# Edge stage of a graph network on Trainium2: groups of six whole buckets instead of 512 slots, and row numbers turned by TensorE instead of through memory

## The reference

```python
def _L1_gnn_ref(h, row, col, dist, eW1, eb1, eW2, eb2, nW1, nb1, nW2, nb2):
    edge_in = jnp.concatenate([h[row], h[col], dist], axis=1)
    e = jax.nn.silu(edge_in @ eW1 + eb1)
    e = jax.nn.silu(e @ eW2 + eb2)
    agg = jax.ops.segment_sum(e, row, num_segments=h.shape[0])
    node_in = jnp.concatenate([h, agg], axis=1)
    out = jax.nn.silu(node_in @ nW1 + nb1) @ nW2 + nb2
    return out
h = jnp.maximum(_layernorm(x, axis=-1), 0.0)
x = x + _L0_gnn_ref(h, edge_index, L0_gnn_W1, L0_gnn_b1, L0_gnn_W2, L0_gnn_b2)
h = jnp.maximum(_layernorm(x, axis=-1), 0.0)
x = x + _L1_gnn_ref(h, src, dst, edge_weight1, ...)
```

## Time and profile before

| what | number |
| --- | --- |
| median of three runs | 9332.65 us |
| profiled execution | 9347.07 us |
| its span in the trace | 9345.3 us |
| mean granted clock of TensorE | 0.972 |
| TensorE busy | 8577.7 us (92%) |
| TensorE, weight loads | 7679.0 us (82%) |
| VectorE busy | 7760.4 us (83%) |
| ACT busy | 5344.2 us (57%) |
| GpSimd busy | 2985.7 us (32%) |

### The profile page before, as it was taken

How to read it: one execution, slowest core, us unless ns; L and a number is a source line. 1 busy time by engine, 2 the same in 40 slices (tenths; PEclk the granted TensorE clock), 3 DMA queues, 4 the chain that set the end, 5 groups by cost and what they waited for, 6 DMA issues and landing times. The chain is left out here.

```text
span 9345.3 us, 289343 instructions
## 1 busy us (share of the span) xinstructions
PE 8577.7 (92%) x95106; PEld 7679.0 (82%) x95890; DVE 7760.4 (83%) x21596; ACT 5344.2 (57%) x14224; POOL 2985.7 (32%) x4177
## 2 busy tenths in 40 slices
PE   3999999999999989998888999599999999999997
PEld 2777777777777769998888998489989899999895
DVE  8999999999999976775888886478888888888884
ACT  3777777777777750001777786245555555555552
POOL 5877777777777830000000000011111111111110
PEclk9999999999999999997999998599999999999998
DMA  2666666666666677664999997533333333333332
GB/s 74 149 150 149 152 148 152 148 151 148 151 148 151 149 172 193 190 190 114 228 222 211 240 241 168 129 98 92 97 93 92 97 91 97 93 94 97 89 97 72
DMA packets 1475613, 1312.43 MB, mean 140 GB/s; under 512 B 829932, under 2 KB 1211094, under 8 KB 1473636
## 3 DMA queue, kind: packets, MB, share of 16 engines
q1 hardware_dynamic: 1444438, 1270.13, 56.3%
q0 software_dynamic: 28224, 26.62, 1.1%
q10 hardware_dynamic: 1840, 0.53, 0.0%
HBM read 777.40 MB, written 361.77 MB: 122 GB/s over the span
## 5 line engine op out<-in xcount | busy, mean ns | idle before, releaser
L621 POOL TENSOR_SCALAR OH<-iot,kd 128x102 bf16<-128x102 bf16 x3440 | 2334.1, 698 | 61.7 <-PE S L753 61.4
L2170 POOL DMA_INDIRECT Qx<-tab_q,tidx x294 | 407.5, 1386 | 5231.9 <-DVE skt L2204 2602.0
L1425 PE MATMUL wp<-AF,XS 128*128 128x256 f32 x9604 | 1214.6, 285 | 157.5 <-issue 121.7
L1425 PEld LDWEIGHTS wp<-AF,XS 128*128 128x128 f32 x9604 | 1165.9, 191 | 189.0 <-issue 188.8
L911 ACT ACTIVATE RB<-PS 128x256 int16<-128x256 f32 x2401 | 898.6, 381 | 639.9 <-PE PS L779 591.6
L1451 ACT ACTIVATE AF<-RG 128x1536 fp32r<-128x1536 uint8 x686 | 1022.6, 1491 | 340.9 <-PE wp L1425 208.0
L794 PE MATMUL HP<-T3a,RB 128*128 128x193 bf16 x9604 | 1187.3, 246 | 27.3 <-ACT RB L911 27.3
L753 PE MATMUL S<-LH,OHf 128*102 128x256 f32 (+14 forms) x6860 | 1160.5, 316 | 50.3 <-ACT LH L875 29.6
L2191 ACT ACTIVATE Z<-Zb 128x512 f32<-128x512 f32 x882 | 556.2, 631 | 991.6 <-DVE Zb L2249 987.6
L875 ACT ACTIVATE LH<-LB,pl 128x128 f32<-128x128 bf16 (+14 forms) x4116 | 1113.1, 356 | 0.0
L753 PEld LDWEIGHTS S<-LH,OHf 128*102 128x102 f32 x6860 | 921.7, 169 | 195.9 <-issue 96.1
(11 more groups left out here) (329 smaller groups left out, 16065.5 us busy)
## 6 DMA issues: line engine op xcount, KB each, us to landing
RG<-adjT SPq DMA_DIRECT2D x1372, 224.0 KB, 7.0
adj<-RB SPq DMA_DIRECT2D x343, 448.0 KB, 2.8
adjT<-RT SPq DMA_DIRECT2D x686, 224.0 KB, 3.7
RG<-adj SPq DMA_DIRECT2D x686, 224.0 KB, 4.6
sdb<-bk SPq DMA_DIRECT2D x196, 768.0 KB
sdb<-bk SPq DMA_DIRECT2D x98, 384.0 KB
sdb<-bk SPq DMA_DIRECT2D x98, 261.0 KB
WR<-wk SPq DMA_DIRECT2D x882, 9.0 KB
```

Source lines behind the costliest of these rows:

```text
L621: ins = e.tensor_scalar(OH[:, g * GT + k, :], iot1[:, 0:KEYS], kd[:, g * GT + k:g * GT + k + 1], None, ALU.is_equal)
L1425: ins = e.matmul(ps[b][:, 0:256], lhsT=XS[:, n * PB + m, :, :].rearrange("p c f -> p (c f)"), rhs=AF[:, (b + n) % 3, m, :], start=n == 0 a ...
```

## The change

A group is now six whole buckets, `GW` = 504 places, in groups 0 to 7, and 512 in the ninth; a block has `SLOTS` = 8 x 504 + 512 = 4544 places, and `NX` = 284 of them, in `NXT` = 4 pieces of 71, are for late records. A group of 504 is cut into four tiles that start at steps of `TW` = 126 places and are 128 wide; so two places of each tile lie in the next one too. `skt` takes 126 numbers per tile (the last two rows stay zero and match nothing), so that a place counts once. The tiles of the ninth group are 128 apart; so `skt` is loaded with two transfers. The widths of `WR`, `Pb`, `Y` and `OsT` become 506 in groups 0 to 7. `xti` is now fp32 (`xtf`), `tix` is gone, and four transposes on TensorE and one copy on VectorE write `tidx` at the end of the unpacking. `SPACE2` goes from 52 to 114.

```diff
-SLOTS = 4608
+GW = 6 * SLB
+NGB = 9
+TW = GW // 4
+SLOTS = (NGB - 1) * GW + 512
 NX = SLOTS - AT_X
-NXT = 3
+NXT = 4
-SPACE2 = 52
+SPACE2 = 114
-NTL = SLOTS // P
+NTL = NGB * 4
...
                     e.wait_ge(x_v, 13)
-                    e.dma_start(tix.rearrange("b t n -> b (t n)"), xti[0:BLK, :]).then_inc(o_s, 16)
...
                     spaced(e, SPACE2)
                     e.wait_ge(x_v, 14)
+                    for t in range(NXT):
+                        e.transpose(pxt[0:XT, t * P:(t + 1) * P], xtf[:, t * XT:(t + 1) * XT], idn[:, :])
                     e.matmul(pov[:, 0:1], lhsT=onef[:, :], rhs=xov[:, 0:1], start=True, stop=True).then_inc(x_v, 1)
...
+                    step(e.tensor_copy(tidx[0:XT, :, :].rearrange("n b t -> n t b"),
+                                       pxt[0:XT, :].rearrange("n (t b) -> n t b", b=P)[:, :, 0:NBK]))
...
-                    with nc.allow_non_contiguous_dma(reason="34104 row numbers, once"):
-                        e.dma_start(tidx[0:XT, :, :].rearrange("n b t -> n (b t)"), tix.rearrange("b t n -> n (b t)")).then_inc(o_s, 16)
...
-            PWD = GPP * 512
+            PWD = GPP * GW
+            PLN = PWD + 512 - GW
...
+            def wide(g):
+                return 512 if g % GB9 == GB9 - 1 else GW + P - TW
+            def tile_at(t, g):
+                return t * (P if g % GB9 == GB9 - 1 else TW)
...
             def buckets_of(g):
-                at = g % GB9 * 512
-                return [(c,) + span(c * SLB, c * SLB + SLB, g) for c in range(at // SLB, min(NCH, (at + 511) // SLB + 1))]
+                c = g % GB9 * 6
+                return [(t,) + span(t * SLB, t * SLB + SLB, g) for t in range(c, min(NCH, c + 6))]
...
-                                e.dma_start(skt[q][0:NTL, :], bk[DS(k, 1), 0, :].rearrange("a (t n) -> (a t) n", n=P)).then_inc(l_sd[q], 16)
+                                e.dma_start(skt[q][0:NTL - 4, 0:TW], bk[DS(k, 1), 0, 0:SLOTS - 512].rearrange("a (t n) -> (a t) n", n=TW)).then_inc(l_sd[q], 16)
+                                e.dma_start(skt[q][NTL - 4:NTL, :], bk[DS(k, 1), 0, SLOTS - 512:SLOTS].rearrange("a (t n) -> (a t) n", n=P)).then_inc(l_sd[q], 16)
...
-                            e.matmul(pT[g % 2][:, :], lhsT=WB[:, :], rhs=WR[j][:, at:at + 512], start=True, stop=True)
+                            e.matmul(pT[g % 2][:, 0:wide(g)], lhsT=WB[:, :], rhs=WR[j][:, at:at + wide(g)], start=True, stop=True)
...
-                                e.matmul(o[:, :], lhsT=Pb[q][:, c, :], rhs=S_[:, :], start=False, stop=True, skip_group_check=True)
+                                e.matmul(o[:, 0:wide(g)], lhsT=Pb[q][:, c, :], rhs=S_[:, 0:wide(g)], start=False, stop=True, skip_group_check=True)
...
-                                ins = e.matmul(p2[g % 2][:, t * P:(t + 1) * P], lhsT=Y[g % 2][:, t * P:(t + 1) * P], rhs=nW["eW2s"][:, :],
+                                ins = e.matmul(p2[g % 2][:, t * P:(t + 1) * P], lhsT=Y[g % 2][:, tile_at(t, g):tile_at(t, g) + P], rhs=nW["eW2s"][:, :],
...
-                            e.activation(Y[g % 2][:, :], pT[g % 2][:, :], ACT.Silu, bias=nW["eb1s"][:, 0:1]).then_inc(l_y, 1)
+                            e.activation(Y[g % 2][:, 0:wide(g)], pT[g % 2][:, 0:wide(g)], ACT.Silu, bias=nW["eb1s"][:, 0:1]).then_inc(l_y, 1)
...
-                            ins = e.tensor_scalar(OsT[g % 2][:, :], v[:, 0, at:at + 512], pio[:, 0:1], None, ALU.is_equal)
+                            ins = e.tensor_scalar(OsT[g % 2][:, 0:wide(g)], v[:, 0, at:at + wide(g)], pio[:, 0:1], None, ALU.is_equal)
```

More of the change, by code:

```diff
@@ L1561, in gnn_kernel @@
             xsi = sbt(vx, "xsi", [P, NX], i32)
-            xti = sbt(vx, "xti", [P, NX], i32)
+            xtf = sbt(vx, "xtf", [P, NX], fp32)
             xsb = sbt(vx, "xsb", [P, NX], bf16)
@@ L1568, in gnn_kernel @@
             pov = pst(vx, "pov")
+            pxt = pst(vx, "pxt")
             x_v = sem("x_v")
@@ L1582, in _ @@
                     e.wait_ge(s_wb, 48)
-                    e.wait_ge(o_s, 48)
+                    e.wait_ge(o_s, 32)
                 @block.tensor
@@ L1625, in _ @@
                     step(e.tensor_scalar(och[:, :], och[:, :], 9, None, ALU.arith_shift_right))
-                    step(e.scalar_tensor_tensor(xti[:, :], och[:, :], 256.0, xci[:, :], ALU.mult, ALU.add))
+                    step(e.scalar_tensor_tensor(xtf[:, :], och[:, :], 256.0, xci[:, :], ALU.mult, ALU.add))
                     step(e.tensor_copy(half(xwf[:, :], NX, 1), half(found[1][:, :], NX, 0)))
@@ L1993, in gnn_kernel @@
             GPP = 3
-            PWD = GPP * 512
+            PWD = GPP * GW
+            PLN = PWD + 512 - GW
             LR = (64, 64, 80)
-            sdb = [sbt(cx, f"sdb{n}", [P, 2, PWD], bf16) for n in range(3)]
-            WR = [sbt(cx, f"WR{n}", [P, PWD], bf16) for n in range(3)]
+            sdb = [sbt(cx, f"sdb{n}", [P, 2, PLN], bf16) for n in range(3)]
+            WR = [sbt(cx, f"WR{n}", [P, PLN], bf16) for n in range(3)]
             skt = [sbt(cx, f"skt{n}", [P, P], bf16) for n in range(2)]
@@ L2039, in span @@
             def span(a, b, g):
-                at = g % GB9 * 512
-                return max(a - at, 0), min(b - at, 512)
+                at = g % GB9 * GW
+                return a - at, b - at
             def buckets_of(g):
-                at = g % GB9 * 512
-                return [(c,) + span(c * SLB, c * SLB + SLB, g) for c in range(at // SLB, min(NCH, (at + 511) // SLB + 1))]
+                c = g % GB9 * 6
+                return [(t,) + span(t * SLB, t * SLB + SLB, g) for t in range(c, min(NCH, c + 6))]
             def regular(g):
-                return min(512, AT_D - g % GB9 * 512)
+                return min(GW, AT_D - g % GB9 * GW)
             with nc.Block() as block:
@@ L2112, in stage_t @@
                             if g % GB9 == 0:
-                                e.wait_ge(l_sd[q], i * 16 + (16 if g >= 0 else 0))
+                                e.wait_ge(l_sd[q], i * 32 + (32 if g >= 0 else 0))
                                 e.wait_ge(l_sk, i * 2 + (q + 1 if g >= 0 else q - 1))
@@ L2224, in onehot @@
                                 ins = e.tensor_scalar(OdT[g % 2][:, h, 0:wd], v[:, 1, at:at + wd], pio[:, h:h + 1], None, ALU.is_equal)
-                            if wd < 512:
+                            if wd < GW:
                                 a, b = span(AT_D, AT_X, g)
```

10 lines of the change are left out of this document (4 added, 6 removed).

## The result

Four runs of the changed kernel took 9192.38 to 9234.14 us, median 9223.65; four of the kernel before 9325.49 to 9351.01, median 9339.89. The ratio is 0.987 with a 95% interval of 0.985 to 0.9889: 1.1 to 1.5% faster, some 116 us. The forecast was 9242 (9190 to 9280), a gain of 90. The profiled execution took 9234.14 us, its span 9232.3, which is 113.0 us less than before.

A forecast was written before the change was run, and what follows sets the result against it. The prediction took TensorE's matmul list in the edge stage as the bound. Its terms, -90 (parts 1 to 3), -8.4 (part 4) and +8 (part 5), sum to -90 us, from 9332.65 to 9242; range 9190 to 9280, own range 9225 to 9265.

The forecast's parts named there:

- TensorE's list bounds the edge stage: Edge stage: TensorE, busy 97%, sets the pace; shortening its list shortens the stage 98 times over while VectorE keeps idle time.
- Its own signs: Profile after: `pS` 30.6 us apart, 36-matmul rows 1.52 us, `p` step 111 ns; wrong unless turnless blocks are 0.9 us shorter.
- ACT's hole: Table stage: ACT's 14.06 us idle before the fourth `Pst`, waiting for `tab_p`, would be gone, its 4.70 us steps unbroken.
- Part 1, the cuts: Edge stage: no bucket cut, 48 matmuls fewer per block; 0.86 us gained, 0.07 back, net 0.79 us a block.
- Parts 2 and 3: Edge stage: fewer late-record columns in the ninth group, 0.07 us; narrower `WR` and `Pb`, 0.06 us a block.
- Part 4: Table stage: row numbers no longer go through memory, so `tab_n` and `tab_p` go sooner; -8.4 us, bounds 0 and -11.4.
- Part 5, the loop head: TensorE's edge loop branch: the turn becomes dearer by 0.17 us, +8 us in all, bounds -34 and +50.
- the loop turn becomes cheap: Edge loop: rival that the turn's cost, dependent on place and time, goes, -34 us, giving 9200; chance 0.2.
- the low end: Whole kernel: 9190 us, the low end of the forecast range, set under the cheap loop.
- the unaligned weight loads of `Y`: `stage_2`: rival that fp32 weight loads at steps of 504 bytes are slower, up to 564 us, 9,800; chance 0.04.
- VectorE stays beneath TensorE: Edge stage: VectorE keeps about 0.5 us idle a group; rival that it or ACT's chain becomes the bound, 9325, chance 0.06.

The follow-up runs named there:

- e11: Changed kernel with one bucket of each group of 504 cut in two again, loop placed at 66: ratio 0.9928, median 9284.63 us.
- e7: Kernel before with only the row numbers changed: three transposes and a copy replace the store and load of `tix`; ratio 0.9985.
- e9: Kernel before with 183 increments instead of 52, so its loop of 2,034 entries starts 66 behind a multiple of 256: ratio 0.9967.
- e2: Changed kernel with 244 increments instead of 114, so its loop starts 205 behind a multiple of 256: ratio 0.987, as the changed kernel.
- e5: Kernel before with 164 increments instead of 52, so its loop starts 47 behind a multiple of 256: ratio 1.0028.
- e6: Changed kernel with 284 increments instead of 114, so its loop starts 245 behind a multiple of 256: ratio 0.9892.
- e1: Changed kernel with 52 increments instead of 114, so its loop starts 13 behind a multiple of 256: ratio 1.0158.
- e8: Changed kernel with 190 extra fp32 matmuls in TensorE's wait ahead of the node MLP: 9220.92 to 9222.41 us, ratio 0.9874.

## Why the prediction was right, and where it was wrong

- **TensorE's list bounds the edge stage:** right. It is 99.8% busy, and nothing took its place.
- **Its own signs:** the eight rows of 36 matmuls take 1.53 us for the 1.52 worked out, the `p` step is still 111 ns and ACT's hole is gone. But `pS` starts 30.38 us apart instead of 30.6, and a block without a turn got 0.79 us shorter instead of 0.92, though the prediction had called itself wrong if that weren't 0.9.
- **Part 1, the cuts:** right in kind, a little too large: 0.86 us for the eight cuts. Between the starts of the two kernels' matmuls (medians of all blocks) the eight rows from first to last start shrink by 0.90 us, and the next matmul then starts 12 ns later behind 84 columns than behind a short piece, eight times: 0.80 us, and 0.75 with e11's order of pieces. The step that failed is "since the longer tail lies under the next matmul, up to 0.88 us": the last matmul's columns do push the next one back. The estimate of 0.74 that the formula of the Trainium skill gave (TensorE: Matmul & The Clock Gate, "Wait — 56ns, not 53.3ns?") lies as near on the other side.
- **Parts 2 and 3:** by the same starts the ninth group stays as long as it was, as forecast (0.07 us back and 0.07 us gained), and the narrower `WR` and `Pb` give 0.07 us (forecast 0.06). Not foreseen: `Pb` waits for `OdT` (0.05 us a block, last section), and 0.02 us between p and `Pb`. In all 0.80 + 0.07 - 0.05 - 0.02 = 0.80 us; a block without a turn lost 0.79 in the medians (31.15 to 30.37). 0.79 x 98 = 77 us; forecast were 90, and 77 is just under the lower bound of 80.
- **Part 4:** -8.4 forecast, 8.5 in e7. In the changed kernel the way from the layer norm to the first `pS` is 183.5 us (6070.3 - 5886.80), 6.2 less than before. Up to the last `Pst` it saves the forecast 8.4 us (156.55 for 164.93); from there to the first `pS` it takes 2.2 us more (26.9 for 24.7). The wider `Qx` to clear is 0.3 of that, and VectorE waits 2.0 us longer for the first `WR` (10.02 for 8.06), of which the second `skt` load explains 0.5; the rest stays open. The text had set both against a saving of 0.6 us ahead of the stage. That at 71 places the old path would have cost 125 us was not seen.
- **Part 5, the loop head:** wrong, and the largest error: +8 us forecast, about -35 measured (e9 alone: 34.5). The step that failed is "the branch comes to stand 136 behind a border. The fetch that the border starts then has 0.7 us less time". It took for granted that each turn fetches its instructions. It was the rival "the loop turn becomes cheap", at a chance of 0.2, but not for the reason given there. The turns without loss, from which the text argued, were turns whose nine packets were hidden, not turns without a fetch. The row to ask was the count of packets: 386 in 2,700 us of the stage are nine for each turn, as many as the blocks it touches, and 2,034 entries are one block short of that. The Trainium skill (Runtime: NRT & Kernel Launch, "Instruction fetch mechanics") gives TensorE room for 2,048 instructions in blocks of 256; the runs agree with that number. Its sentence that a taken branch out of the current two blocks must fetch, which the prediction quoted and set aside, does not hold here: a branch back over eight blocks fetches nothing (e2, e9). The turns without loss, for which the prediction had set it aside, don't speak against it, since they fetched.
- **The sum:** -77 - 35 - 6 = -118 for the parts; the layer norm also began 10.2 us earlier (5886.80 for 5897.04), which it did in e5 too (5886.72), the kernel before with other increments, while in e6, the changed kernel with other increments, it began at 5900.99; so it is no work of the change, and the node MLP lost 12.9 us to the clock. -118 - 10 + 13 = -115, measured -113.0. That the forecast gain is only 26 us short is in part luck: the cuts were taken for 13 us too much and the turn for 43 too little, and the clock took back 13 us that no term held. Without the low end, which was set by the rival of the cheap turn, the measured 9223.65 would lie just outside the forecast's own 9225 to 9265.
- **Rivals:** the unaligned weight loads of `Y` cost nothing (275 ns a pass and 1.05 us for eight, as before); VectorE stays beneath TensorE, but see below.

## What to carry to other kernels

Count the packets of instructions in a loop before you argue about its branch: if there is one for each block of 256 entries a turn, the loop is fetched anew each time, and bringing it into eight blocks, by its length or by its place, takes the turn's whole cost away. Place it with room on both sides, since ten entries too far cost 266 us here, where nine fetched blocks a turn had cost the kernel before 34 us. A transfer of single elements should be judged by its rate with the partition count it will have, and a pause of TensorE ahead of a stage by the clock it leaves behind.

## What the runs showed of the hardware that was not expected

- **Partitions and DMA:** 71 places instead of 116 cut the pace of 4-byte elements to a quarter (170 for 658 packets per us). The gathers of `Qx` show the same kind of effect: with 116 rows each made 96 packets in its queue (28,224 for 294), with 71 rows 208 (81,536 for 392), and one takes 1.95 us of GpSimd for 1.39. 116 is a multiple of 4 and 71 a prime number, and four times fewer packets were under way at once; that the divisor is the reason was not tried.
- **GpSimd and VectorE:** once a block a comparison of VectorE takes over three times its time while GpSimd issues the gathers. Timeline of the changed kernel (start, length):

```profile
8076.88 2.26 POOL L2183 DMA_INDIRECT Qx<-tab_q,tidx  x1 [0.30 <-issue]
...
8077.77 1.47 DVE L2237 TENSOR_SCALAR OdT<-sdb,pio 128x504 bf16<-128x504 bf16 x2
...
8079.30 0.30 PEld L2133 LDWEIGHTS pT<-OsT,Pb 128*128 128x128 f32 x2
```

The two `OdT` of 504 columns take 1.47 us (0.60 in the other groups) while a gather is at work: one of the two takes 1.21 us instead of 0.34. From 6200 to 9000 us none of the 924 comparisons that overlap no gather takes over 0.35 us. `Pb` follows right behind, and in every second block the way from `Pb` to the buckets takes 0.1 us more. The kernel before has a smaller case of it: there it is `OsT` that takes up to 0.85 us for 0.48 while a gather is at work, and `OdT` keeps its 0.35. This is the first sign of what would bound the stage next.
- **The clock costs as much as code:** by their timelines the second linear stage took 71 us in the changed kernel (5768.9 to 5840.2) and 40 us in e1 (5772.1 to 5811.9), and the node MLP some 13 us more or less (215.1 us behind the last `pS`, 201.3 in e8), by whether the clock fell around a pause ahead of them. That is as much as lies between the fastest and the slowest run of the changed kernel, 42 us.
